# Decoder layer: the second head's scores moved behind the gate products, and scores times values taken by heads in place of blocks

## The reference

```
qkv    = silu(hidden @ qkv_w.T)                    # 32 heads, q, k, v of 128 each
scores = (q @ k.T) * decay                         # decay: 0 for later tokens
attn   = scores @ v
normed = norm_w * attn * rsqrt(mean(attn**2) + eps)
gate   = sigmoid(hidden @ gate_w.T)
x      = x + (gate * normed) @ out_w.T
```

## Time and profile before

| | us |
|---|---|
| median of 3 runs | 2106.26 (2105.53 to 2108.85) |
| the profiled execution | 2104.41 |
| its span, first to last instruction | 2102.6 |
| TensorE busy | 2061.6, 98% of the span |
| VectorE, ScalarE, GpSimd busy | 1394.5, 1131.9, 755.0 |

### The profile page before, as it was taken

How to read it: one execution, slowest core, us unless ns; L and a number is a source line. 1 busy time by engine, 2 the same in 40 slices (tenths; PEclk the granted TensorE clock), 3 DMA queues, 4 the chain that set the end, 5 groups by cost and what they waited for, 6 DMA issues and landing times.

```text
span 2102.6 us, 42522 instructions
## 1 busy us (share of the span) xinstructions
PE 2061.6 (98%) x16208; PEld 1692.6 (81%) x16208; DVE 1394.5 (66%) x1993; ACT 1131.9 (54%) x1936; POOL 755.0 (36%) x882
## 2 busy tenths in 40 slices
PE   5999999999999999999999999999999999999998
PEld 5788888888888888888888888888888888666665
DVE  5566656566666566776666665666666656788885
ACT  4545555454555455555555554545455554666664
POOL 5433425252434343643444342525343433211110
PEclk9999999999999999999999999999999999999999
DMA  2211111111212111111111111111120111311110
GB/s 83 92 62 42 57 48 52 52 52 41 64 31 67 38 53 44 50 43 47 57 42 62 41 51 51 51 48 54 36 66 30 62 41 56 131 34 50 52 38 21
DMA packets 40547, 110.23 MB, mean 52 GB/s; under 512 B 4960, under 2 KB 9568, under 8 KB 40288
## 3 DMA queue, kind: packets, MB, share of 16 engines
q1 hardware_dynamic: 40272, 107.78, 16.1%
q10 hardware_dynamic: 144, 0.52, 0.1%
HBM read 104.09 MB, written 4.19 MB: 52 GB/s over the span
## 4 chain that ended last, share of the span: by engine, by line
PE 95%; DVE 3%; ACT 1%; issue 0%; POOL 0%; DMA 0%; POOLq 0%; DVEq 0%
PE bank L1160 15%; PE bank L1165 14%; PE bank L1163 14%; PE bank L1225 6%; PE bank L1226 5%; PE bank L1227 5%; PE bank L1188 5%; PE bank L1193 5%; PE bank L1191 5%; PE bank L1215 4%; PE bank L1203 3%; PE bank L1566 3%; PE bank L1579 3%; PE bank L212 2%; PE bank L1605 1%; PE bank L1588 1%
## 5 line engine op out<-in xcount | busy, mean ns | idle before, releaser
L552 POOL TENSOR_TENSOR raw<-raw 128x256 f32<-128x256 f32 x128 | 127.2, 994 | 604.1 <-DMA raw<-w_pairs 604.1
L1160 PE MATMUL bank<-x_hi,w_hi_c 128*128 128x512 f32 x672 | 267.0, 397 | 2.1 <-DVE v L906 1.8
L1165 PE MATMUL bank<-x_hi,w_lo_c 128*128 128x512 f32 x672 | 262.1, 390 | 0.0
L1163 PE MATMUL bank<-x_lo,w_hi_c 128*128 128x512 f32 x672 | 261.8, 390 | 0.0
L1225 PE MATMUL bank<-wo_hi,y_hi 128*128 128x512 f32 x512 | 202.1, 395 | 1.6 <-DVE y_lo L948 1.3
L1226 PE MATMUL bank<-wo_lo,y_hi 128*128 128x512 f32 x512 | 199.8, 390 | 0.0
L1227 PE MATMUL bank<-wo_hi,y_lo 128*128 128x512 f32 x512 | 199.4, 390 | 0.0
L583 POOL TENSOR_TENSOR sq_acc<-sq_acc,sq 128x512 f32<-128x512 f32 x124 | 161.7, 1304 | 92.8 <-ACT sq L748 83.8
L906 DVE TENSOR_TENSOR qk<-bank,qk 128x512 f32<-128x512 f32 x192 | 127.2, 689 | 85.1 <-ACT qk L719 42.6
L1160 PE MATMUL bank<-x_hi,w_hi_a 128*128 128x512 f32 x448 | 176.0, 393 | 0.0
L1165 PE MATMUL bank<-x_hi,w_lo_a 128*128 128x512 f32 x448 | 174.5, 389 | 0.0
(11 more groups left out here) (182 smaller groups left out, 5390.1 us busy)
## 6 DMA issues: line engine op xcount, KB each, us to landing
raw<-w_pairs SPq DMA_DIRECT2D x127, 512.0 KB, 3.6
raw<-w_out SPq DMA_DIRECT2D x32, 512.0 KB, 3.5
xr<-x SPq DMA_DIRECT2D x4, 1024.0 KB, 7.5
raw<-ctx_in SPq DMA_DIRECT2D x16, 256.0 KB, 2.9
raw<-ctx_in SPq DMA_DIRECT2D x32, 128.0 KB, 3.1
out<-attn_acc SPq DMA_DIRECT2D x16, 256.0 KB, 2.0
attn_acc<-x SPq DMA_DIRECT2D x8, 256.0 KB, 6.4
decays<-decay SPq DMA_DIRECT2D x32, 64.0 KB, 3.0
```

What stands on the lines that cost most here:

```text
L552: nc.gpsimd.tensor_tensor(raw[:, S1], raw[:, S3], raw[:, A22], ALU.add).then_inc(done, 1)
L1160: nc.tensor.matmul(bank[:, to], w_hi[w][:, a, s], x_hi[:, b, c], start=part in ("first", "only") and c == 0, stop=False, skip_group_check= ...
L1163: nc.tensor.matmul(bank[:, to], w_hi[w][:, a, s], x_lo[:, b, c], start=False, stop=False, skip_group_check=True)
L1165: i = nc.tensor.matmul(bank[:, to], w_lo[w][:, a, s], x_hi[:, b, c], start=False, stop=part in ("last", "only") and c == 1, skip_group_che ...
```

## The change

The scores of a pair's second head are made after the gate products and directly before scores times values; `weigh` goes head by head (both blocks of h=0, then both of h=1) and waits for each head's scores only when it comes to it. The first tile is on the full width for (h=0, b=0), (h=0, b=1) and (h=1, b=0). VectorE decays the second head's scores after its work for the gates. Two POOL steps and one SP wait move with it.

```diff
@@ sync
             for n in range(1, TB):
                 cross.load_x(sp, n)
+            sp.wait_ge(scores_ready, 2 * QUADS * 4)
             sp.dma_start(cross.eye[:, :, :], cross.eye_in).then_inc(cross.S["eye_landed"], 16)
@@ gpsimd
-                if half == 0 and at(d, LAST):
-                    token_sums(1, 2)
                 if following:
                     mix0(half, d, 6)
                 if half == 0 and at(d, LAST):
+                    token_sums(1, 2)
                     token_sums(1, 3)
@@ vector
+                project_gate(half, d, G01, lambda: cut_out(half, d, 0))
                 decay_scores(half, d, 0, 1)
-                project_gate(half, d, G01, lambda: cut_out(half, d, 0))
...
-                decay_scores(half, d, 1, 1)
                 if before_turning:
                     normalise(2)
                 project_gate(half, d, G23, lambda: cut_out(half, d, 1))
+                decay_scores(half, d, 1, 1)
@@ tensor
-            def weigh(half, d, s, b):
+            def weigh(half, d, s):
                 for h in range(HG):
-                    for i in range(TT):
-                        first = (s * HG + h) * HD
-                        wide = HD if h == i == 0 else SEQ
+                    pe.wait_ge(scores_ready, count(half, d, 4, 2 * s + h + 1))
+                    for b in range(2):
+                        for i in range(TT):
+                            first = (s * HG + h) * HD
+                            wide = HD if i == 0 and (h == 0 or b == 0) else SEQ
...
+                pe.wait_ge(w_b, count(half, d, 4, 4))
+                pe.wait_ge(silu_ready, count(half, d, 18, 12))
+                project(half, d, G01, 1)
                 pe.wait_ge(scores_ready, count(half, d, 4, 1))
                 make_scores(half, d, 0, 1)
-                pe.wait_ge(w_b, count(half, d, 4, 4))
-                project(half, d, G01, 1)
-                pe.wait_ge(c22_ready, count(half, d, 6, 2))
-                pe.wait_ge(scores_ready, count(half, d, 4, 2))
                 if previous:
                     pe.wait_ge(out_added, count(half, d, 16, 0))
-                weigh(half, d, 0, 0)
-                weigh(half, d, 0, 1)
+                weigh(half, d, 0)
...
+                pe.wait_ge(w_c, count(half, d, 6, 6))
+                pe.wait_ge(silu_ready, count(half, d, 18, 18))
+                project(half, d, G23, 2)
                 pe.wait_ge(scores_ready, count(half, d, 4, 3))
                 make_scores(half, d, 1, 1)
-                pe.wait_ge(w_c, count(half, d, 6, 6))
-                project(half, d, G23, 2)
-                pe.wait_ge(scores_ready, count(half, d, 4, 4))
                 pe.wait_ge(out_added, count(half, d, 16, 8))
-                weigh(half, d, 1, 0)
-                weigh(half, d, 1, 1)
+                weigh(half, d, 1)
```

More of the change, by code:

```diff
@@ L1205, in make_scores @@
                 k.then_inc(s_mm, 1)
-            def weigh(half, d, s, b):
+            def weigh(half, d, s):
                 for h in range(HG):
-                    for i in range(TT):
-                        first = (s * HG + h) * HD
-                        wide = HD if h == i == 0 else SEQ
[L1212 to L1219, removed]
+                    pe.wait_ge(scores_ready, count(half, d, 4, 2 * s + h + 1))
[3 more added lines that the diff above has]
+                            wide = HD if i == 0 and (h == 0 or b == 0) else SEQ
+                            for top in range(2):
+                                keys, to = slice(top * SEQ, (top + 1) * SEQ), (h * TT + i) * SEQ
+                                for c in range(0, HD, wide):
+                                    k = nc.tensor.matmul(bank[c:c + wide, y_bank[b][top], to:to + SEQ],
+                                                         v[keys, b, i, first + c:first + c + wide],
+                                                         scores[keys, h, b * TT + i], start=True, stop=True)
+                                if h == HG - 1 and i == TT - 1:
+                                    k.then_inc(pv_mm, 1)
             def project_out(half, d, s, i):
```

## The result

The changed kernel takes 2141.0 us (median of 4 runs, 2138.0 to 2141.7) against 2106.4 for the kernel before: a ratio of 1.0159, with a 95% interval of 1.0147 to 1.0171. It is slower by 34.6 us where 31.8 were forecast, inside the range. The profiled execution took 2140.8 with a span of 2139.0.

The account below looks back on a forecast made before the run. TensorE was taken to bound the kernel, its delays in the quads reaching the end one for one. The terms -7.0 + 13.1 + 25.7 gave +31.8 us, so 2138 us, with a range of 2128 to 2150.

Parts of the forecast that it names:

- gates in front of scores: Per pair, TensorE no longer goes from scores into gates and gates into `weigh`: 0.22 us saved, 7.0 us in all.
- third wide start: Inside `weigh`, one more full-width tile per pair costs 0.41 us over quadrants: 13.1 us more.
- chain, pair 0: Behind `weigh`, ahead of QK2: block 0 completes later, so ScalarE's snapshot delays product n=2 by 0.84 us: 13.5 us.
- chain, pair 1 ahead of VA: Same delay behind pair 1's `weigh`: 0.73 us in 12 quads, 0.87 in two without room: 10.5 us.
- chain, the other two pairs: At the end of half 0 and the last of all: 0.87 us each at most, taken as 1.7 us.
- Counting changes of mode at 0.11 us each: Alternative count of TensorE's tiling switches, 7 per pair before and 8 after: 3.5 us more instead of 6.1.
- a room of 0.14 us: Slack between snapshot's end and product n=2 of VA, in the common case, taken to absorb part of the delay.
- Costs at nothing: New wait in `weigh`, gates' earlier needs, SP's later loads and the `eye` load: all taken as covered, 0 us.
- The second head's wait: Inside `weigh`, for the second head's decayed scores: covered by 0.86 us, cost taken as 0, 1.6 us at most.
- wide starts did cost: Against the rival that by heads they run on without gaps in `weigh`: -5 us, 2101 us, chance 0.04.
- VectorE was in time: Against the rival that TensorE waits for the second head's scores: 10 to 25 us on top, 2148 to 2163, chance 0.08.
- The first rival: Behind `weigh`, the snapshot doesn't hold TensorE up: only +6.1 us, 2112 us, chance 0.07.

Follow-up runs that it names:

- kernel with two wide starts: Changed kernel, by heads, with the wait for the second head moved up to the first head's block 1 and that head starting on quadrants: 2127.6 us.
- the one with four: Changed kernel with one more wide tile, at the second head's block 1, behind block 0's end: 2139.7 us.
- the same TensorE list with a shorter chain: Changed kernel with ScalarE's squares of block 1 moved behind its first snapshot of the next projection, VectorE's gate behind its first sum: 2117.6 us.
- more or less work on TensorE behind block 0's end: Two runs: changed kernel with a wide tile added at the second head's block 1, 2139.7 us; kernel before with block 1 begun on quadrants, 2104.9 us.
- the kernel by blocks in the new place: Changed kernel with the loops of `weigh` turned back to blocks, second head's wait at its first tile of block 0, still three wide starts: 2112.2 us.
- two edits of no measurable effect alone: On the kernel before: one wide start per pair, 2104.9 us; block 1's squares and gate moved late, 2106.3 us; both together, 2090.8 us.
- kernel by heads in the old place: Kernel before with only `weigh` changed, to go by heads with three wide starts; scores stay where they were: 2145.4 us.

## Why the prediction was right

Sums of distances from start to start, the changed kernel against the one before:

| step of the prediction | forecast us | in the traces us |
|---|---|---|
| gates in front of scores | -7.0 | -5.5 |
| third wide start | +13.1 | +13.3 |
| chain, pair 0 | +13.5 | +15.0, of which about 1.1 is a fall of the clock |
| chain, pair 1 ahead of VA | +10.5 | +11.9 |
| chain, the other two pairs | +1.7 | +1.1, all that is left over |
| first quad, a fall of the clock | not foreseen | +0.6 |
| the profiled execution | +31.8 | +36.4 |

**What bounds the kernel.** Right: from one `weigh` to the next the changed kernel is about 1.1 us longer in nearly every pair, as the steps sum up, and all of it is found again in the end. No large errors cancel in the sum. The extra loss is in the terms that follow and in two falls of the clock (last section).

**Spacing.** G01 went from 9.74 to 9.61 us, and nothing was paid for going from scores straight into `weigh`: scores take 1.08 us in either neighbourhood. The forecast 7.0 us came down to 5.5. Half of the difference is G23 of half 0's last quad, which took 10.72 us, and 10.06 before. (G01 of that quad took 9.88, and some G23 of the loop 9.63 to 9.71.) In that G23, as the timelines of ScalarE and TensorE show, the output weights had only just landed for ScalarE, and its snapshot came too late for a product:

```profile
915.58 1.35 ACT L687 ACTIVATE wo_hi<-raw,normw 128x512 fp32r<-128x512 f32 x2 [1.22 <-DMA raw<-w_out]
```

```profile
918.58 0.51 PE L1160 MATMUL bank<-x_hi,w_hi_c 128*128 128x512 f32 x1 [0.77 <-ACT gate L694]
```

I had looked at the first snapshot of the gates only, not at the loads that their being 1.08 us early overtakes. The profile of the changed kernel shows ScalarE waiting for this load in 15 of the 16 quads (1.22 us here, 0.3 to 0.9 us in the others), that of the kernel before in none. Only here did it cost TensorE much; elsewhere G23 grew by 0.1 us at most.

**The third wide start.** Right in size (0.41 us a pair) and in place. The kernel with two wide starts gives the wide tile as the cause, the one with four shows that its price reaches the kernel's time only ahead of block 0's end, as long as the chain holds. Counting changes of mode at 0.11 us each, as I weighed it, would have given half: the two changes around a wide tile and the tile itself come to 0.41. The Trainium skill (TensorEngine Tiling (Array Packing), Key Properties) says that TensorE drains at a change of the tiling mode; the traces agree in kind, with 0.41 us for such a tile, but no run here separates the drain from the rest of that price.

**The chain.** Right, and shown from both sides: the same TensorE list with a shorter chain (-23.5 us), and more or less work on TensorE behind block 0's end with no effect (2139.7; 2104.9). Behind pair 0 and ahead of VA the term was 1.8 us too small, once the fall of the clock is taken off. For VA I had taken a room of 0.14 us from the distance of snapshot and product; the projection grew by 0.85 and not by 0.73, since a product that really waits also spoils the step behind it (0.22 against 0.12 us in VA, 0.34 against 0.31 in QK2).

**Costs at nothing.** The second head's wait was free even with the cover cut to 0.07 us (two wide starts). SP's longer wait, the later load of QK1's weights and the `eye` load appear in no wait of TensorE. The gates in front were not free: see G23 above.

**Rivals.** The chain did hold; wide starts did cost; VectorE was in time. The first rival's price, 2112, is met by the kernel by blocks in the new place, 2112.2, in which the chain is covered while the other two terms stand.

## What to carry to other kernels

Where one engine bounds the kernel, count not only its own list but the point in it at which a result becomes complete, and follow the first consumer back to the bounding engine: a reordering of equal work that completes the first half later costs exactly that delay, if the chain behind it has no room. Compare iterations in which the same wait holds the engine with those in which it doesn't: a constant distance between release and start gives the tie away before anything idles. And if an edit that shortens the bounding engine's list changes nothing, look for such a tie before the edit is thrown away: here two edits of no measurable effect alone are worth 0.7% together.

## What was not expected of the hardware

TensorE's granted clock fell to half (1.2 of 2.4 GHz) for 3.4 us in the first quad of the changed kernel's profiled execution, behind a stretch in which TensorE was busy for 3.88 of 6 us and had just waited 1.78 us for VectorE. The rows of the windows give the stretch and its length, busy us and count of PE, PEld, DVE, ACT and POOL, then the granted clock, the DMA's share and GB/s. The first two are of this fall and the third of the one at 1790 us; TensorE's timeline follows:

```profile
50.00:56.00 6.00, 3.88 (x27) 3.35 (x27) 4.13 (x6) 1.80 (x3) 1.29 (x1) 1.00 0.10 27
56.00:60.00 4.00, 4.00 (x12) 3.15 (x11) 0.51 (x1) 1.55 (x2) 1.96 (x3) 0.57 0.97 326
1790.00:1794.00 4.00, 4.00 (x12) 3.14 (x11) 2.56 (x5) 3.37 (x6) 3.19 (x3) 0.57 0.01 2
```

```profile
54.95 0.47 PE L1160 MATMUL bank<-x_hi,w_hi_c 128*128 128x512 f32 x1 [1.78 <-DVE v L906]
...
56.69 0.63 PE L1160 MATMUL bank<-x_hi,w_hi_c 128*128 128x512 f32 x1
57.12 0.63 PE L1163 MATMUL bank<-x_lo,w_hi_c 128*128 128x512 f32 x1
```

Steps went from 0.23 to 0.43 us, and QK0 of that quad took 12.8 us in place of 11.2. The net loss against the kernel before was less, 0.6 us at the scores behind it, for QK0 had begun a microsecond earlier. The instructions of this stretch are the same in the kernel before, whose profile has no such fall; of the nine experiments' profiles five have it (QK0 takes 12.8 us in them) and four have not (11.2), without regard to what was edited. So I take it as varying from execution to execution. A second fall, at 1790 us behind the last `sums`, cost about 1.1 us (QK2 there took 11.24 us, against 10.15 in the kernel by heads in the old place); the kernel with four wide starts has it too. What decides either was not tried.

Unexpected too was the price of a wait just met: a matmul that really waited starts 0.05 us behind its release, and the step behind it is 0.1 us longer (0.34 instead of 0.23 us with 512 columns, 0.22 instead of 0.12 with 256). So a tie shows in the spacing although the profile counts no idle time for it: the earlier trace rows and the second quad of the earlier trace rows have no bracket.
